# One expert stage, three changes in the order of its queues: the gate half's own announcement, later residual sums, later mixing jobs

## The reference, cut to what matters

```python
xn = layernorm(x)
x = x + L3_attn(xn, ...) + L3_ffn(xn, ...)

# L3_ffn: 64 small experts, 8 of them weighted per token, and a shared one; H = 128, I = 64
affinity = sigmoid(xn @ router_w); top 8, weights w = scores / sum
gate_out = einsum('bsh,ehi->bsei', xn, expert_gate_k)
up_out   = einsum('bsh,ehi->bsei', xn, expert_up_k)
routed   = einsum('bsei,eih->bsh', silu(gate_out) * up_out * mask, expert_down_k)
# L3_attn: token shift, five mixed inputs, low-rank tanh gates, a decaying state per head
#   (S = exp(w_t) * S + k_t v_t), group norm, a silu gate, an output projection
```

## Time and profile before

| what | value |
|---|---|
| time, median of 3 (lowest to highest) | 4510.52 us (4507.15 to 4515.63) |
| the profiled execution | 4513.74 us |
| its span in the trace | 4511.9 us |
| TensorE, VectorE, ScalarE, GpSimd busy, of the span | 88%, 75%, 65%, 50% |
| mean granted TensorE clock | 0.956 of full speed |

### The profile page before, as it was taken

One profiled execution on the slowest core, in us unless ns is written; L12 is line 12 of the kernel. 1 busy time (PEld: TensorE's weight loads), 2 busy tenths in 40 slices (PEclk: granted clock), 3 DMA queues, 4 the chain that ended last, 5 costly groups with the idle time before them and its releaser, 6 DMA issues. The chain is left out here.

```text
span 4511.9 us, 88013 instructions
## 1 busy us (share of the span) xinstructions
PE 3976.7 (88%) x34586; PEld 2220.9 (49%) x34588; DVE 3397.3 (75%) x4741; ACT 2913.5 (65%) x4403; POOL 2235.9 (50%) x1443
## 2 busy tenths in 40 slices
PE   6999999999998989996788877897888868998998
PEld 3667666766666654451112211345777443333333
DVE  6888888888884557767988899466777746788777
ACT  3777777777776449963777677784566724544544
POOL 2888878888885013330221110371666535544554
PEclk7999999999999989996999999898999989999999
DMA  3212212212220011100220100241000324444443
GB/s 83 58 39 58 58 40 55 58 48 49 58 49 1 1 48 71 59 17 24 71 76 21 42 24 15 88 132 58 12 15 14 101 90 108 111 112 113 100 119 99
DMA packets 113913, 270.28 MB, mean 60 GB/s; under 512 B 24276, under 2 KB 36308, under 8 KB 111004
## 3 DMA queue, kind: packets, MB, share of 16 engines
q1 hardware_dynamic: 98084, 223.86, 18.5%
q0 software_dynamic: 15424, 40.89, 2.7%
HBM read 178.10 MB, written 50.81 MB: 51 GB/s over the span
## 5 line engine op out<-in xcount | busy, mean ns | idle before, releaser
L522 POOL TENSOR_TENSOR a_prob_low<-a_prob_whole,a_prob_high 128x1024 f16<-128x1024 f32 x512 | 1084.4, 2131 | 277.0 <-ACT a_prob_high L412 274.3
L496 DVE TENSOR_REDUCE a_part_max<-a_top 128x2 f32<-128x1024 f32 x512 | 626.1, 1223 | 218.4 <-PE a_top L323 212.5
L409 ACT ACTIVATE a_prob_whole<-a_score 128x1024 f32<-128x1024 f32 x512 | 524.9, 1025 | 332.3 <-PE a_score L312 320.4
L976 ACT ACTIVATE a_prob<-a_score 128x512 f32<-128x512 f32 x1024 | 533.1, 604 | 262.6 <-PE a_score L915 262.6
L1009 DVE TENSOR_REDUCE a_part_max<-a_side 128x2 f32<-128x1024 f32 x512 | 594.9, 1218 | 70.4 <-PE a_side L886 70.4
L412 ACT ACTIVATE a_prob_high<-a_score 128x1024 f16<-128x1024 f32 x512 | 522.3, 1020 | 0.0
L2182 POOL TENSOR_TENSOR m_lows<-m_scaled,m_high 128x512 f16<-128x512 f32 x264 | 308.9, 1172 | 359.2 <-ACT m_high L2145 342.7
L311 PE MATMUL a_score<-a_qa,a_ka 128*128 128x256 f16 x2048 | 476.2, 273 | 0.0
L312 PE MATMUL a_score<-a_qb,a_kb 128*128 128x256 f16 x2048 | 476.0, 273 | 0.0
L378 PE MATMUL a_o_ps<-a_v,a_prob_high 128*128 128x65 f16 x4096 | 428.1, 193 | 6.2 <-POOL a_prob_low L522 3.4
L380 PE MATMUL a_o_ps<-a_v,a_prob_high 128*128 128x64 f16 x4096 | 426.9, 194 | 0.0
(11 more groups left out here) (478 smaller groups left out, 10124.8 us busy)
## 6 DMA issues: line engine op xcount, KB each, us to landing
m_gate<-gates SPq DMA_DIRECT2D x264, 256.0 KB, 5.2
a_ka<-a_nat_high_k SPq DMA_DIRECT2D x128, 128.0 KB, 2.4
e_gate<-gates SPq DMA_DIRECT2D x8, 2048.0 KB, 7.2
slots<-in_slots SPq DMA_DIRECT2D x19, 520.0 KB, 4.2
a_qa<-a_nat_high_q SPq DMA_DIRECT2D x64, 128.0 KB, 2.4
a_qa<-a_nat_low_q SPq DMA_DIRECT2D x64, 128.0 KB, 2.4
a_qb<-a_nat_high_q SPq DMA_DIRECT2D x64, 128.0 KB, 2.4
a_kb<-a_nat_low_k SPq DMA_DIRECT2D x64, 128.0 KB, 2.4
```

The costliest lines, as they stand in the source:

```text
L409: eng.activation(prob_whole[:, e % RING, :, :, :], score[:, e % 2, :, :, :], ACT.Exp, scale=scale)
L496: eng.tensor_reduce(part_max[:, i, c, :, qt % 4], top[:, :, :], AX.X, ALU.max).then_inc(max_done, 1)
L522: eng.tensor_tensor(prob_low[:, e % RING, :, :, :], prob_whole[:, e % RING, :, :, :], prob_high[:, e % RING, :, :, :], ALU.subtract).then_ ...
L976: eng.activation(prob[:, e % RING, h, :], score[:, step % SLOTS, :], ACT.Exp).then_inc(exp_done, 1)
```

## The change

Three edits, all inside `mixing_and_experts`. First, a new semaphore `upper_full`: `hidden_step` waits for `weighted` of step s-2, makes the gate half and announces `hidden_full`; then it waits for `upped` of step s-2, makes the up half and announces `upper_full`, for which the second multiply now waits in addition. Second, VectorE's residual sum moves from ahead of the slot's two multiplies to behind them, ahead of the slot's mixing jobs. Third, ScalarE's mixing jobs move from the head of their slot to its end, behind silu and the high part.

```diff
+        upper_full = pl.sem("upper_full")
...
                     if s >= HB:
+                        eng.wait_ge(weighted, s - HB + 1)
+                    x = [part[:, c * BANK:(c + 1) * BANK] for part in (x_high, x_low)]
+                    product(hidden[:, s % HB, :], 3 * j, n % 2, x, True, True).then_inc(hidden_full, 1)
+                    if s >= HB:
                         eng.wait_ge(upped, s - HB + 1)
-                    x = [part[:, c * BANK:(c + 1) * BANK] for part in (x_high, x_low)]
-                    product(hidden[:, s % HB, :], 3 * j, n % 2, x, True, True)
-                    product(upper[:, s % HB, :], 3 * j + 1, n % 2, x, True, True).then_inc(hidden_full, 1)
+                    product(upper[:, s % HB, :], 3 * j + 1, n % 2, x, True, True).then_inc(upper_full, 1)
...
-                    for name, c in act_jobs[slot]:
-                        mix(name, c)
                     if 2 <= slot < 2 + BANKS:
...
                         eng.activation(high[:, s % HR, :], scaled[:, s % SR, :], ACT.Copy).then_inc(high_done, 1)
+                    for name, c in act_jobs[slot]:
+                        mix(name, c)
...
-                    s = step_at(slot, LAG + 1)
-                    if s >= 0 and s % J == J - 1:
-                        eng.wait_ge(out_used, s + 1)
-                        add_to_res(s % PER_UNIT // J, out[:, :], summed, s // J + 1)
                     s = step_at(slot, UP_LAG)
...
                         eng.wait_ge(weighted, s + 1)
+                        eng.wait_ge(upper_full, s + 1)
                         eng.tensor_tensor(scaled[:, s % SR, :], acted[:, :], upper[:, s % HB, :], ALU.mult).then_inc(upped, 1)
+                    s = step_at(slot, LAG + 1)
+                    if s >= 0 and s % J == J - 1:
+                        eng.wait_ge(out_used, s + 1)
+                        add_to_res(s % PER_UNIT // J, out[:, :], summed, s // J + 1)
```

## The result

| what | before | after |
|---|---|---|
| time, median of 4 (lowest to highest) | 4513.08 us (4507.15 to 4516.37) | 4473.94 us (4469.48 to 4475.59) |
| ratio after to before, 95% interval | | 0.9913 [0.9896, 0.993] |
| profiled execution; span | 4513.74; 4511.9 | 4475.59; 4473.8 |
| the loop, first to last start of `acted` | 759.4 | 719.3 |

The changed kernel is 39 us faster; 27 were forecast. It leaves out what the earlier stages vary by (the first `acted` starts between 3736.6 and 3753.8 us in the runs told here).

A forecast was written before the change was run, and what follows sets the result against it. TensorE was taken to bound the last stage's loop. Saving 3.65 us per chunk gives 25.6 over seven chunks, plus about 1.5 in the first: 27 us off the 4510.5 median, stated as 4484, range 4470 to 4498.

The forecast's parts named there:

- The bound: Last stage's loop: TensorE is the bound and loses 83 us standing still, 54.5 us of waits ended by `scaled`.
- The flaw to see: VectorE waits 66.3 us at the residual sum, ready multiplies queued behind it, and TensorE then waits for these multiplies.
- step 15's multiplies: Entry to slots 16 to 28: they no longer stand behind the sum, 1.4 us, so the stretch starts earlier.
- Slots 9 to 15: ScalarE's jobs behind silu end slot 11's 1.24 us stall; with the sum's new wait in slot 13, 0.8 us saved.
- Slots 16 to 28: VectorE is the bound at 9.38 us per three slots; reordering saves only 0.15 a turn; the stretch starts earlier.
- scan theory: Experiments' theory: a third or more of the gain comes from scans no longer held by GpSimd's low part.
- The added wait: VectorE's wait on `upper_full` ahead of the second multiply: 0.06 us per step, 0.6 us per chunk.
- more is won: Rival, chance 0.15: added wait free, sums in slots 1, 13 and 28 meet VectorE earlier; about 50 us saved, 4460.
- Slots 29 to 4: Earlier stalls mostly go, new ones of 1.3 us at `z` and in slot 1; slot 5 starts another 1.3 us ahead.
- The exit at slot 28: The last sum has two multiplies in front, so the down product of slot 28 waits about 0.5 us more.
- `rep`: Copy of `keys`, at most some 2 us later; its transfer still ends before the scan needs it, with little left.
- slower, through `summed`: Rival, chance 0.11: late sums stop TensorE at each of 88 down products; at 1.3 us each, 4563 us.

The follow-up runs named there:

- e2: Kernel before with only the residual sums moved behind the multiplies: 4528.40 us, ratio 1.0025.
- e7: Kernel before with the gate half announced on its own, both halves still waiting for the second multiply: 4482.27 us, ratio 0.9927.
- e8: Kernel before with the gate half waiting only for the first multiply, silu still after all six matmuls: 4480.95 us, ratio 0.9927.
- e1: Kernel before with only the split announcement (both its halves): 4473.72 us, ratio 0.9905.
- e5: Kernel before with GpSimd's low part started only after the scan in slots 17, 20, 23 and 26: 4501.22 us, ratio 0.9973.
- e6: Split and ScalarE's order, sums in the old place, plus a GpSimd filler ahead of the low part in four slots: 4468.15 us, ratio 0.9905.

## Why the prediction was right, and where it was not

**The bound: right.** The lost time stood at TensorE's wait for `scaled`. With the split that wait is 0.2 us or none, and the loop is 40 us shorter.

**The flaw to see: there, but not the one to mend.** The sum at the head of the queue did make multiplies late: moving it alone takes TensorE's wait for them from 50.0 to 26.1 us. But 31.0 us at the sum come in their place, with a lower clock behind them, and the kernel is slower. With the sum in its old place and the other two edits made, VectorE idles there as long as before (67.5 us), and the kernel is faster still: the split takes the wait for the multiplies away without moving the sum. The sums' move was forecast to pay in the long stretch, and on the kernel before it does: slots 16 to 28 shrink by 1.30 in e2, where 1.4 was put on step 15's multiplies, though some 0.5 of it is shorter scans and `u` (0.52 a chunk). But with the split already there it costs 0.63 in that stretch (36.14 to 36.77), 0.89 in slots 9 to 15 and 0.25 after 29. The waits that were forecast, "some 20 to 30 us", are there at 24.3. What was missing is that without the move TensorE would lose hardly anything in their place.

**Slots 9 to 15: the sum right (0.66 for 0.8), the cause wrong.** The step gave the stall of slot 11 to ScalarE's order. With that order alone the stretch takes 17.89 for 17.99: the stall is only spread over slots 11 and 12. Timeline of TensorE in that kernel, first matmuls of the two slots:

```profile
4218.67 0.39 PE L1972 MATMUL m_up_down<-m_x_high,m_w_high 128*128 128x512 f16 x1 [0.23 <-DVE m_scaled L2304]
...
4222.26 0.39 PE L1972 MATMUL m_up_down<-m_x_high,m_w_high 128*128 128x512 f16 x1 [0.62 <-DVE m_scaled L2304]
```

With the split alone the stretch falls to 16.33. In the mean of the six chunks slot 11 follows slot 10 after 3.34 us in the kernel before, 2.68 with the announcement alone (e7), 2.54 with the release alone (e8) and 2.08 with both (e1), where the bare pace is 1.94: the split takes 1.26 of the 1.40 by itself. The new wait in slot 13 was put at 0.83 and is 1.03.

**Slots 16 to 28: the step that failed, and the main reason for 39 in place of 27.** "Here VectorE is the bound, and reordering saves only that 0.15 a turn": VectorE was the bound, but its 9.38 us a turn were not fixed. The turn from 4242.44 to 4251.82 holds the scan at 4245.23, 2.15 us long, that takes 1.28 when GpSimd's low part is out of its way. An estimate from the runs: the scans and `u` of a chunk go from 11.89 us to 9.81 with the change, and 0.92 of these 2.08, as in e5 and e6, is 1.9 us a chunk, some 13 of the 40 us of loop. So the scan theory's third is about right. With the forecast 1.55 and the 0.65 that were put down for the added wait and did not come, the stretch should have won 4.1; it won 3.30. Of the 0.8 between, 0.35 lies at the entry (the first scan comes 1.11 earlier after the start of slot 16, in the mean; 4236.06 less 4233.8, less 0.8, is 1.46) and 0.18 at the exit; the rest is open.

**The added wait: mis-sized.** It was put at 0.06 us a step, within 0 and 0.12. First to second multiply takes 0.78 with it and 0.79 without: nothing, neither the 0.6 us a chunk nor the 0.5 to 1.0 that was estimated beside it. The traces have the reason. In 260 of the 264 steps of either kernel one semaphore instruction stands ahead of the second multiply. Before, it holds the wait for the first multiply; after, that wait and the new one together, so no further instruction came in. The 0.06 between the 0.73 and the 0.79 of the earlier trace rows is there only where it holds the wait for the first multiply: in the first four steps of the changed kernel it holds the wait for `upper_full` alone, and they take 0.72 and 0.73. The "more is won" rival named this half of it; its other half, cheap waits for the sum, did not happen.

**Slots 29 to 4: right in size.** `z` was to cost 1.3 and costs 1.28, the down product of slot 1 was to cost 1.3 and costs 1.13; 1.48 saved for 1.3. The runs add whose gain it is: the split alone loses 0.91 there, and ScalarE's order is worth 0.35 by itself and 2.64 once the split is in place, since it keeps the wait for `z` short and the clock up. The prediction had no term for the clock; in the whole change it needed none.

**The exit at slot 28** was to cost 0.5 at the down product and costs 0.68. **`rep`** was to be covered, and is. The rival "slower, through `summed`" had the sign of this one edit right; it asked for 0.69 us at each of eleven down products of a chunk before all would be lost, and 15.1 us over 88 are 0.17.

**The total: in part luck.** 4473.94 us lies within the 4470 to 4498 of the forecast. But some 13 us of gain from the scans were not foreseen, and the sums' move, which was to pay, cost 15.1; the two nearly cancel.

## What to carry to other kernels

Before an engine is called the bound of a stretch with a fixed time per turn, look whether the same instruction has two durations in the trace and what runs beside the long ones: here 2.15 and 1.28 us for one scan stood for an estimated third of the gain. Idle time of an engine at a wait is a reason to reorder its queue only if more is late behind that wait than will be late for what is moved back: here 23.9 us went at the multiplies and 31.0 came at the sum. An edit that lets the waiting engine need less, as the split does, comes first. Of a change with several parts run the parts: here one part made the whole gain, one paid only on top of it, and one cost 15 us that the total hid. Read the granted clock of each such run too: by estimate two thirds of what ScalarE's order seemed to win on the split, and of what the sums' move seemed to cost alone, was the clock behind a longer wait.

## What the runs showed of the hardware

A scan on VectorE whose inputs `rep` and `kv` both lie in SBUF (`pl.sb` in the kernel) stands still, but for some 0.2 us, while GpSimd's low part runs, if that began first: 1.94 and 2.15 us where 0.86 and 1.07 of the low part were left, 1.28 when clear. If the scan begins first, GpSimd's operation is held: the one at 4210.69 takes 1.79 in place of 1.16. `u`, whose inputs are in SBUF too, goes from 0.75 to 0.97 or 0.98 in 25 of 32 cases of the kernel before, and to 1.70 in e5; the multiply after it, one of whose inputs is a matmul's output in PSUM (`work`, `pl.ps`), takes 0.69 in all 32, whether GpSimd works beside it (6 of 32) or not.

The Trainium skill, SBUF — State Buffer, section Who interferes with whom, says that a VectorE instruction with two SBUF inputs contends with a GpSimd instruction that reads SBUF, and that the order of issue decides which of the two blocks. The trace agrees in both directions, with the durations just given.

A semaphore instruction ahead of a VectorE instruction holds one or two waits here. The second of two, for a value that had arrived, cost nothing (0.78 us from first to second multiply, 0.79 with one).

TensorE's granted clock is 1.00 through both loops that were compared, but for the first 0.8 us of the changed one. It falls to 0.50 for 3.4 us behind six of seven waits of 2.15 to 2.37 us in e1 and behind six waits of 2.27 to 3.32 us in e2. Behind others it stayed up: 2.76 us, ended at 4444.5, in the changed kernel.
